# A non-local block in split float32: one row of K's weights moves by 64 bytes, and K takes that row first and last

## The reference

```python
q = einsum('bchw,dc->bdhw', x, theta_w) + theta_b         # 256 planes, 1024 places
xpool = maxpool2(x)                                       # 256 places
k = einsum('bchw,dc->bdhw', xpool, phi_w) + phi_b
v = einsum('bchw,dc->bdhw', xpool, g_w) + g_b
p = softmax(einsum('bdn,bdm->bnm', q, k) * hp ** (-0.5))  # hp = 256
vp = einsum('bdm,bnm->bdn', v, p)
out = einsum('bdhw,cd->bchw', vp, z_w) + z_b + x
```

## Time and profile before

| | us |
|---|---|
| median of 3 runs (2054.66 to 2056.37) | 2055.68 |
| the profiled execution | 2058.26 |
| its span, first to last instruction | 2056.5 |

### The profile page before, as it was taken

One profiled execution on the slowest core, in us unless ns is written; L12 is line 12 of the kernel. 1 busy time (PEld: TensorE's weight loads), 2 busy tenths in 40 slices (PEclk: granted clock), 3 DMA queues, 4 the chain that ended last, 5 costly groups with the idle time before them and its releaser, 6 DMA issues.

```text
span 2056.5 us, 49021 instructions
## 1 busy us (share of the span) xinstructions
PE 2033.3 (99%) x17804; PEld 2030.3 (99%) x17804; DVE 1555.1 (76%) x2623; ACT 1299.0 (63%) x2228; POOL 1369.3 (67%) x830
## 2 busy tenths in 40 slices
PE   8999999999999999999999999999999999999997
PEld 8999999999999999999999999999999999999997
DVE  7787777787777877777877778777778777787765
ACT  6667666666566666666665666666666656667653
POOL 4577666776666776677766667766777666677643
PEclk9999999999999999999999999999999999999999
DMA  7555556656556555566465665565664655665625
GB/s 231 200 188 201 198 177 216 232 172 211 175 210 225 190 197 202 175 215 237 169 211 175 208 224 194 194 205 173 215 238 170 211 175 206 224 196 192 208 103 182
DMA packets 212907, 407.27 MB, mean 198 GB/s; under 512 B 12688, under 2 KB 15760, under 8 KB 212880
## 3 DMA queue, kind: packets, MB, share of 16 engines
q1 hardware_dynamic: 212736, 406.90, 58.3%
q10 hardware_dynamic: 144, 0.01, 0.0%
HBM read 272.64 MB, written 134.22 MB: 198 GB/s over the span
## 4 chain that ended last, share of the span: by engine, by line
PE 96%; DVE 1%; DMA 1%; POOL 1%; issue 1%; ACT 0%; SPq 0%; DVEq 0%; POOLq 0%
PE bank L863 96%; DMA x<-x 1%; DVE x_top L688 0%; POOL x_split_lo L548 0%; DVE pt_raw L670 0%; DVE x_bot L688 0%; DVE pooled L642 0%; POOL att_lo L566 0%; PE bank L870 0%; ACT att_hi L392 0%; POOL att_f L561 0%; SPq L252 0%; ACT probs L453 0%; DVE xp_lo L785 0%; ACT att_f L382 0%
## 5 line engine op out<-in xcount | busy, mean ns | idle before, releaser
L548 POOL TENSOR_TENSOR x_split_lo<-x,x_split_hi 128x1024 fp32r<-128x1024 f32 x255 | 613.8, 2413 | 252.8 <-ACT x_split_hi L353 229.6
L863 PE MATMUL bank<-x_split_hi,theta_hi 128*128 128x256 f32 x2048 | 566.2, 276 | 3.0 <-DVE x_split_lo L720 2.4
L863 PE MATMUL bank<-x_split_hi,theta_lo 128*128 128x256 f32 x2048 | 566.1, 276 | 0.0
L863 PE MATMUL bank<-x_split_lo,theta_hi 128*128 128x256 f32 x2048 | 566.1, 276 | 0.0
L863 PE MATMUL bank<-att_hi,z_hi 128*128 128x256 f32 x1792 | 495.6, 277 | 6.0 <-DVE x_bot L688 3.4
L863 PE MATMUL bank<-att_hi,z_lo 128*128 128x256 f32 x1792 | 494.8, 276 | 0.0
L863 PE MATMUL bank<-att_lo,z_hi 128*128 128x256 f32 x1792 | 494.8, 276 | 0.0
L670 DVE STREAM_TRANSPOSE pt_raw<-probs 32x256 f32<-32x256 f32 x1024 | 445.8, 435 | 17.4 <-ACT probs L453 0.8
L688 DVE TENSOR_TENSOR x_top<-bank,x_top 128x512 f32<-128x512 f32 x512 | 334.8, 688 | 72.0 <-PE bank L863 67.8
L863 PEld LDWEIGHTS bank<-x_split_hi,theta_hi 128*128 128x128 f32 x2048 | 385.1, 188 | 3.5 <-issue 3.5
L566 POOL TENSOR_TENSOR att_lo<-att_f,att_hi 128x768 fp32r<-128x768 f32 x191 | 281.6, 1480 | 159.0 <-ACT att_hi L392 159.0
(11 more groups left out here) (74 smaller groups left out, 4401.5 us busy)
## 6 DMA issues: line engine op xcount, KB each, us to landing
x<-x SPq DMA_DIRECT2D x256, 512.0 KB, 3.9
x_top<-x SPq DMA_DIRECT2D x128, 512.0 KB, 7.0
x_bot<-x SPq DMA_DIRECT2D x128, 512.0 KB, 5.2
out<-x_top SPq DMA_DIRECT2D x128, 512.0 KB, 3.6
out<-x_bot SPq DMA_DIRECT2D x128, 512.0 KB, 6.6
x_top<-theta_wt SPq DMA_DIRECT2D x4, 256.0 KB, 5.8
x_top<-g_wt SPq DMA_DIRECT2D x4, 256.0 KB, 6.7
x_bot<-z_wt SPq DMA_DIRECT2D x4, 256.0 KB, 7.1
```

The costliest lines, as they stand in the source:

```text
L548: nc.gpsimd.tensor_tensor(flat(lo), flat(x_chunk(s, c)), raw(flat(hi)), ALU.subtract).then_inc(x_ready, 1)
L863: last = nc.tensor.matmul(dst, stationary(a), moving(b), start=start and n == 0, stop=stop and n == len(PRODUCTS) - 1, skip_group_check=re ...
```

## The change

The low part of phi becomes one flat tensor that is 64 bytes (16 float32) longer, and its last row, kt = 7, starts 64 bytes further on. `phi_block` gives K the place of a block. K takes row 7 first for the columns of m = 0 and last for those of m = 1; before, it was last in both. VectorE makes phi's low part row by row, with two instructions per piece in place of one. `still` has 176 columns instead of 192, 32 bytes less. All that is declared behind phi starts 64 bytes later.

```diff
-STILL = 192
+STILL = 176
+SHIFT = 16
...
-        phi = [sb(f"phi_{s}", [P, KT, D], f32r) for s in ("hi", "lo")]
+        phi = [sb("phi_hi", [P, KT, D], f32r), sb("phi_lo", [P, KT * D + SHIFT], f32r)]
...
+        def phi_block(part, kt, m):
+
+            at = kt * D + m * P
+            if part == HI:
+                return phi[HI][:, kt, m * P:(m + 1) * P]
+            at += SHIFT if kt == KT - 1 else 0
+            return phi[LO][:, at:at + P]
...
             def lo_weights(i, p):
                 dve.wait_ge(w_hi, i * PIECES + p + 1)
+                if i == PHI:
+                    for kt in range(KC * p, KC * p + KC):
+                        at = kt * D + (SHIFT if kt == KT - 1 else 0)
+                        last = nc.vector.scalar_tensor_tensor(out=phi[LO][:, at:at + D], in0=staged(i, p)[:, kt % KC * D:(kt % KC + 1) * D],
+                                                              scalar=SCALE, in1=raw(phi[HI][:, kt, :]), op0=ALU.mult, op1=ALU.subtract)
+                    last.then_inc(w_ready, 1)
+                    return
                 nc.vector.scalar_tensor_tensor(out=piece(i, p, LO), in0=staged(i, p),
-                                               scalar=SCALE if i == PHI else 1.0, in1=raw(piece(i, p, HI)),
+                                               scalar=1.0, in1=raw(piece(i, p, HI)),
                                                op0=ALU.mult, op1=ALU.subtract).then_inc(w_ready, 1)
...
             def project_k():
                 for m in range(DT):
-                    for kt in range(KT):
-                        last = product(k_bank[:, m * M:(m + 1) * M], lambda a: phi[a][:, kt, m * P:(m + 1) * P],
-                                       lambda b: xp[b][:, kt, :], kt == 0, kt == KT - 1)
+                    order = (tuple(range(KT)), (KT - 1,) + tuple(range(KT - 1)))[m == 0]
+                    for kt in order:
+                        last = product(k_bank[:, m * M:(m + 1) * M], lambda a: phi_block(a, kt, m),
+                                       lambda b: xp[b][:, kt, :], kt == order[0], kt == order[-1])
                 last.then_inc(k_done, 1)
```

## The result

| | before | after |
|---|---|---|
| median, us (4 runs each) | 2055.26 (2054.66 to 2056.37) | 2089.78 (2086.95 to 2090.20) |
| ratio, 95% interval | | 1.0165 (1.0152 to 1.0178) |
| the profiled execution, us | 2058.26 | 2090.05 |
| its span, us | 2056.5 | 2088.2 |

The forecast was 2049.5 us, 0.3% faster. The kernel became 1.65% slower. The time lies at the upper edge of the range, 2048 to 2091, where the rival "an odd number of switches" stood with 2087.

A forecast was written before the change was run, and what follows sets the result against it. TensorE's matmul pace was taken to bound the kernel. Fast Ks 5.6 us plus start 0.9 less phi's low part 0.3 made 6.2 us less than the 2055.68 us median: 2049.5 us, range 2048 to 2091.

The forecast's parts named there:

- an odd number of switches: Rival: each K turns the pace three times, every other stretch between Ks slow; 2087 us (2084 to 2091), chance 0.23.
- One like pair, one switch, in both directions: Streaming operand and weights loaded beside it starting on the same 64-byte half turn TensorE's pace once, fast or slow.
- a pair that needs the moving operand: Named way to fail: a like pair turns the pace only together with a change of the moving operand.
- two on end that don't cancel: Named way to fail: two like pairs in succession at K's end do not undo each other's switch.
- The two pairs at the end: At K's end, row 7's load and the way out were to cancel, keeping K fast; cost 0 to 0.04 us.
- the start's pair without effect and the end's two cancelling: Converse of the odd rival: one turn in each K, with the same time, 2087 us.
- The fast K was to give back 0.18 us: Each K at the fast pace gains 0.18 us (0.17 to 0.21); 31 Ks give 5.6 us.
- The start: Before the long unbroken stretch: 0.9 us gained by fast matmuls, 0.3 us lost making phi's low part.
- 0.3 us (0 to 0.6) for phi's low part: VectorE's two late pieces, each cut into two instructions before K's start, go from 1.37 to between 1.37 and 1.92 us.
- 0.9 back from matmuls that run fast: If the first K's end doesn't turn the pace, 218 matmuls from 37.26 to 62.88 save 4.3 ns each.
- The early pieces: VectorE's two earlier phi_lo pieces: loss hidden in a 2.27 us wait for x; without that cover, at most 2 x 0.6 us.
- it does nothing to the pace: Rival: shifting weights alone switches nothing in K, end pairs act as one; 2056.0 us (2055 to 2058), chance 0.21.

The follow-up runs named there:

- the pair far from K's ends: Kernel before with 176-column zeros; only phi_lo's block (row 7, m = 1) moved 64 bytes, taken fourth in m = 1; 2053.97 and 2119.70 us.
- two pairs at the start: Changed kernel with early pieces whole and row 6's m = 0 block also on the other half, taken third in K; 2047.66 us, ratio 0.9964.
- without the shift: Changed kernel with its order, zeros and moved tensors, but no row of phi moved and one VectorE instruction a piece; 2054.41 us, ratio 1.000.

## Why the prediction was wrong

**The step that failed** is the sentence "One like pair, one switch, in both directions". The pace isn't a matter of two states but of one fast and three slow ones, and which pair leads where depends on the form it meets. The first row 7 does act (slow-2 to slow-3, slow-1 to fast), but from the fast entry it leads to another slow form, and by their pace the slow forms are alike in all the rows that I had. K's entry, too, is no switch in both directions: it turns fast to slow-2 but leaves slow-1 as it is. So every other K and the 504 matmuls behind it ran at 117.8 ns, 65.02 us from K to K where 62.6 were forecast. Of the two ways to be wrong that the prediction named, a pair that needs the moving operand and two on end that don't cancel, neither was it: the first is refuted by the pair far from K's ends, and the changed kernel's end leaves a fast K fast and a slow one slow. The duration of 188 or 192 ns was in the trace of before, in the weight loads, which I didn't group.

**The two pairs at the end** cancel, as forecast, where K comes fast: the end leaves it fast in the changed kernel and in the one with two pairs at the start. From slow-2 and slow-3 they lead to slow-1; only from slow-1, which the changed kernel never brings to its end, do they lead to fast. So the outcome is the rival's converse, "the start's pair without effect and the end's two cancelling", in its time, though not in its reason. Why two pairs close together don't do what each does alone stays open: from slow-1, one block 64 bytes on gives fast and a plain end then slow-1, yet together they give fast. So does the cause of the forms themselves.

**The sizes were right.** The rival's 504 matmuls at 4.3 to 4.5 ns gave 2.2 us for a slow stretch; the windows give 65.02 - 62.79 = 2.23. The fast K was to give back 0.18 us; 62.79 - 62.62 = 0.17. The rival stood at 2087, the median is 2089.78. What it lacked is the start.

**The start was mis-sized.** Forecast was 0.3 us (0 to 0.6) for phi's low part and 0.9 back from matmuls that run fast. The late halves cost 29.86 - 28.52 = 1.34 us against 1.21, so 0.13, as bounded. The early pieces, given at most 1.2 us, cost 8.84 - 4.38 = 4.46: the 2.27 us of cover went, and with the late halves K starts 2.25 later. The rows to see it by were there: the early pieces took 2226 ns against 684, and I asked how long a half takes, not what an early piece waits for. In the kernels with whole early pieces K starts at 28.0 to 30.3 us. The Trainium skill (SBUF — State Buffer, Who interferes with whom) says that a VectorE instruction with two SBUF inputs and a GpSimd instruction that reads SBUF contend for a port pair that is held exclusively, for the whole instruction, and that a VectorE instruction with one input, outside its two-port modes, does not contend. The trace agrees: 2.62 us for 128x256 with two inputs beside GpSimd, 0.41 without it. The 0.9 us back were there, 218 matmuls between 39 and 63 us for 210. But the start's 264 matmuls still took 33.32 us against 32.79: after a wait of 2.88 us the granted clock was 0.50 from 33 to 36 us (16 matmuls; before 0.76 and 22).

**Right:** that nothing else interrupts TensorE in the long stretch, that order, moved tensors and zeros cost nothing (2054.41 us without the shift), and the shape of the gain, 2047.66 us where K does run fast. The rival "it does nothing to the pace" fell: one block of weights moved by 64 bytes makes 1.65% (2088.48 against 2054.41 us without the shift) and up to 3.2% (2119.70). The rule of the Trainium skill (SBUF — State Buffer, Who interferes with whom) that stood beside it, two independent read ports and an engine that never waits on anyone, doesn't fit these runs as far as speed goes. That the two reads meet is still only argued from the addresses, since no record shows a port.

## What to carry to other kernels

Where TensorE is full, count the matmuls between two fixed points, and group its weight loads as well as its matmuls: a few ns in one of three loads was the only sign of the state that decided 35 us. A pace that lasts has to be followed as a state, from every state that a loop can enter with; two events that look like the same switch need not be one, and a change that keeps a slow entry from healing can have two times. Before an instruction is cut in two, see what each half will wait for: beside a busy GpSimd, a half of a two-input VectorE instruction cost as much as the whole.

## What the runs showed of the hardware

- Float32 matmuls of 128x256 in a row run at 113.3 or 117.8 ns each, and keep the pace over hundreds of matmuls; the slow pace has three forms, told by which of three weight loads takes 192 instead of 188 ns.
- What changes it is a weight load whose start lies otherwise to the moving operand's than those of the loads around it; a move of 64 or 128 bytes acts, one of 256 does not. Whether the distance counts or the weights' start alone isn't told apart. With distance 128 in every pair of K the pace was 118.4 ns, in a pattern of five.
- One program can have two times 3% apart (2053.72 and about 2115.5 us). Three programs did: of one the short execution was profiled, with the loop entered fast, of the other two the long one, with the loop entered slow. That the form at the entry decides is argued from these, since no program has both profiles.
- A two-input VectorE instruction on 128x256 beside a reading GpSimd instruction of 2.58 us lasted 2.62 us, and 0.41 us alone.
